# Float32 transposes and projections of an attention kernel, rewritten as products of 32 columns

## What is computed

```python
# x: (16, 512, 128) float32; H, dk = 16, 8
h = layernorm(x)
Q, K, V = (h @ Wq.T + bq), (h @ Wk.T + bk), (h @ Wv.T + bv)      # split into heads
scores = einsum('bhld,bhrd->bhlr', Q, K) * scale + einsum('bhld,lrd->bhlr', Q, rel_k)
attn = softmax(scores, axis=-1)
out = einsum('bhlr,bhrd->bhld', attn, V) + einsum('bhlr,lrd->bhld', attn, rel_v)
x = x + out @ Wo.T + bo
...
x = x + experts(layernorm(x))        # 2 shared experts, 2 of 8 routed ones
```

## Time and profile before

| | |
|---|---|
| median of 3 runs | 2068.07 us (2067.51 to 2069.0) |
| profiled execution | 2070.57 us, its span 2068.8 us |
| TensorE busy | 2037.4 us, 98% of the span, 37378 matmul records |
| DVE, ACT, POOL busy | 1605.3, 1507.0, 1212.4 us |
| granted TensorE clock, mean | 0.996 |

### The profile page before, as it was taken

The page is one execution under the profiler, slowest core; times in us unless marked ns, Lnnn a source line. Parts: engine busy times, 40 slices in busy tenths (PEclk is TensorE's granted clock), DMA queues, the critical chain, the costliest instruction groups (busy, mean ns, idle before and its releaser), DMA issues.

```text
span 2068.8 us, 86886 instructions
## 1 busy us (share of the span) xinstructions
PE 2037.4 (98%) x37378; PEld 1512.6 (73%) x37378; DVE 1605.3 (78%) x3788; ACT 1507.0 (73%) x3333; POOL 1212.4 (59%) x1283
## 2 busy tenths in 40 slices
PE   5999999999999999999999999999999999999999
PEld 3777777777777777777777777777777777777777
DVE  5877897788778877877897788778886767676765
ACT  3767676777677776667667666666666888888887
POOL 4554464456445544554455446444443898989888
PEclk8999999999999999999999999999999999999999
DMA  4212211221221122112211321223122221222120
GB/s 112 74 54 67 76 48 55 76 65 53 56 80 55 49 66 73 56 46 69 76 53 46 84 67 46 57 73 67 46 54 50 27 31 23 33 27 32 24 30 12
DMA packets 256658, 113.05 MB, mean 55 GB/s; under 512 B 143018, under 2 KB 253492, under 8 KB 256276
## 3 DMA queue, kind: packets, MB, share of 16 engines
q1 hardware_dynamic: 255796, 107.10, 21.3%
q10 hardware_dynamic: 480, 0.39, 0.1%
HBM read 83.34 MB, written 8.39 MB: 44 GB/s over the span
## 4 chain that ended last, share of the span: by engine, by line
PE 91%; DVE 4%; ACT 2%; POOL 1%; issue 1%; DMA 1%; SPq 0%; ACTq 0%; DVEq 0%; POOLq 0%
PE ps L1548 21%; PE ps L1483 12%; PE ps L1568 10%; PE ps L1490 8%; PE ps L1578 8%; PE ps L1501 7%; PE ps L1765 3%; PE ps L1767 3%; PE ps L1766 3%; PE ps L1747 3%; PE ps L1749 3%; PE ps L1748 3%; PE ps L1586 1%; ACT probs L777 1%; PE ps L1464 1%; DVE keys L1235 1%
## 5 line engine op out<-in xcount | busy, mean ns | idle before, releaser
L777 ACT ACTIVATE probs<-ps,neg_max 128x512 f32<-128x512 f32 x1024 | 690.4, 686 | 338.7 <-DVE neg_max L1003 338.6
L1003 DVE TENSOR_REDUCE neg_max<-ps 128x1 f32<-128x512 f32 x1024 | 635.8, 683 | 148.9 <-PE ps L1490 144.8
L549 POOL TENSOR_TENSOR stat_hi<-q_twice,mask8h 128x1024 f16<-128x1024 f16 x128 | 242.6, 1895 | 533.4 <-PE ps L1490 481.7
L1548 PE MATMUL ps<-const,probs 128*128 128x128 f32 x4096 | 497.3, 274 | 1.3 <-ACT probs L777 0.5
L1548 PEld LDWEIGHTS ps<-const,probs 128*128 128x128 f32 x4096 | 454.0, 141 | 29.5 <-issue 15.8
L1008 DVE COPY probs_t<-ps 128x512 f32<-128x512 f32 x512 | 339.9, 684 | 89.8 <-PE ps L1548 87.3
L767 ACT ACTIVATE probs_t<-ps 128x512 f32<-128x512 f32 x512 | 278.8, 595 | 131.8 <-PE ps L1548 129.5
L679 POOL TENSOR_TENSOR probs_t<-probs,probs_t 128x1024 f16<-128x1024 f32 x160 | 341.3, 2156 | 31.1 <-ACT probs_t L859 30.4
L1483 PE MATMUL ps<-keys,stat_hi 128*32 128x512 f16 x4096 | 317.4, 383 | 0.0
L1490 PE MATMUL ps<-rk_split,stat_rel 96*32 96x512 f16 (+2 forms) x4096 | 281.4, 340 | 0.0
L565 POOL TENSOR_TENSOR stat_rel<-q_rel,mask4h 96x1024 f16<-96x1024 f16 x128 | 250.6, 1958 | 49.7 <-PE ps L1490 30.6
(11 more groups left out here) (173 smaller groups left out, 2864.6 us busy)
## 6 DMA issues: line engine op xcount, KB each, us to landing
rv_step<-in_rv_win SPq DMA_DIRECT2D x128, 512.0 KB, 3.9
keys<-keys SPq DMA_DIRECT2D x56, 96.0 KB, 2.7
x_pair<-in_x SPq DMA_DIRECT2D x8, 512.0 KB, 4.4
rel_scratch<-rel_t SPq DMA_DIRECT2D x256, 16.0 KB, 3.2
x_pair<-in_x SPq DMA_DIRECT2D x16, 256.0 KB, 3.1
x_pair<-rel_scratch SPq DMA_DIRECT2D x64, 64.0 KB, 4.3
out<-keys SPq DMA_DIRECT2D x16, 256.0 KB, 2.3
q_twice<-q_hi SPq DMA_DIRECT2D x28, 128.0 KB, 3.0
```

The costliest lines, as they stand in the source:

```text
L777: nc.scalar.activation(probs[:, q, :], ps[:, i, :], ACT.Exp, bias=neg_max[:, q:q + 1], accum_out=row_sum[parity][:, s * QUADS + q:s * QUAD ...
L1003: nc.vector.tensor_reduce(neg_max[:, q:q + 1], ps[:, i, :], op=ALU.max, axis=AX_X, negate=True).then_inc(max_done, 1)
L1548: last = nc.tensor.transpose(ps[:, bank, rt * P:(rt + 1) * P], probs[:, q, rt * P:(rt + 1) * P], ident)
```

## The change

Every float32 transpose of the attention part becomes four float32 products, each with 32 columns of the block as the stationary operand and the identity as the moving one, which write 32 partitions each (new function `transposed`). The three projections are cut in the same way into products of 32 stationary columns: one product of 512 moving columns becomes four of 512, and one of 128 becomes four of 128. The block `rel_o` loses its upper half, which only held zeros, so its transpose is now two products. relative_queries (float16) keeps its transposes, and so do the transposes of the experts' part.

```diff
-        rel_o = sb("rel_o", [P, 4, 32])
+        rel_o = sb("rel_o", [P, 2, 32])
...
+            def transposed(out, rows):
+                for g in range(rows.shape[1] // 32):
+                    last = nc.tensor.matmul(out[32 * g:32 * g + 32, :], rows[:, 32 * g:32 * g + 32], ident, start=True, stop=True, skip_group_check=True)
+                return last
+
             def rows_t(pair, half, bank):
...
-                    last = nc.tensor.transpose(ps[:, bank, t * P:(t + 1) * P], x_pair[:, half * 4 + t, :], ident)
+                    last = transposed(ps[:, bank, t * P:(t + 1) * P], x_pair[:, half * 4 + t, :])
...
-                nc.tensor.matmul(ps[:, bank, :], wk_s[:], xn_t[:, b * L:(b + 1) * L], start=True, stop=True).then_inc(proj_done, 1)
+                for g in range(4):
+                    last = nc.tensor.matmul(ps[32 * g:32 * g + 32, bank, :], wk_s[:, 32 * g:32 * g + 32], xn_t[:, b * L:(b + 1) * L],
+                                            start=True, stop=True, skip_group_check=True)
+                last.then_inc(proj_done, 1)
...
-                    last = nc.tensor.transpose(ps[:, bank, l * D:(l + 1) * D], rows, ident)
+                    last = transposed(ps[:, bank, l * D:(l + 1) * D], rows)
...
-                    last = nc.tensor.matmul(ps[:, bank, t * D:(t + 1) * D], xn_t[:, b * L + t * P:b * L + (t + 1) * P], wv_s[:],
-                                            start=True, stop=True)
+                    for g in range(4):
+                        at = b * L + t * P + 32 * g
+                        last = nc.tensor.matmul(ps[32 * g:32 * g + 32, bank, t * D:(t + 1) * D], xn_t[:, at:at + 32], wv_s[:],
+                                                start=True, stop=True, skip_group_check=True)
...
-                        last = nc.tensor.transpose(ps[:, bank, rt * P:(rt + 1) * P], probs[:, q, rt * P:(rt + 1) * P], ident)
+                        last = transposed(ps[:, bank, rt * P:(rt + 1) * P], probs[:, q, rt * P:(rt + 1) * P])
...
-                nc.tensor.transpose(ps[:, AV_BANK, 3 * P:4 * P], rel_o[:].rearrange("p a r -> p (a r)"), ident).then_inc(rel_tr, 1)
+                transposed(ps[0:64, AV_BANK, 3 * P:4 * P], rel_o[:].rearrange("p a r -> p (a r)")).then_inc(rel_tr, 1)
```

More of the change, by code:

```diff
@@ L275, in attention_ffn @@
         SETUP_FIRST, SETUP_DVE = 6, 9
-        SETUP_POOL = 11
+        SETUP_POOL = 10
         POOL_LINKS = 10
@@ L502, in _ @@
             nc.gpsimd.memset(half_pow[:], -0.5).then_inc(setup_pool, 1)
-            nc.gpsimd.memset(rel_o[:], 0.0).then_inc(setup_pool, 1)
             nc.gpsimd.memset(e_const[:], math.e).then_inc(setup_pool, 1)
@@ L1031, in reduce_relative @@
                 dve.wait_ge(rel_tr, START + pair * STEPS + s)
-                nc.vector.tensor_reduce(rel_o[:, 0:2, :].rearrange("p a (g h) -> p (a g) h", h=DK), r_masked[:].rearrange("p g l h -> p g h l"),
+                nc.vector.tensor_reduce(rel_o[:].rearrange("p a (g h) -> p (a g) h", h=DK), r_masked[:].rearrange("p g l h -> p g h l"),
                                         op=ALU.add, axis=AX_X).then_inc(rel_reduced, 1)
@@ L1438, in project_keys @@
                 pe.wait_ge(xn_t_ready, START + pair * 2 + b + 1)
-                nc.tensor.matmul(ps[:, bank, :], wk_s[:], xn_t[:, b * L:(b + 1) * L], start=True, stop=True).then_inc(proj_done, 1)
+                for g in range(4):
+                    last = nc.tensor.matmul(ps[32 * g:32 * g + 32, bank, :], wk_s[:, 32 * g:32 * g + 32], xn_t[:, b * L:(b + 1) * L],
+                                            start=True, stop=True, skip_group_check=True)
+                last.then_inc(proj_done, 1)
             def project_queries(pair, b, bank):
-                nc.tensor.matmul(ps[:, bank, :], wq_s[:], xn_t[:, b * L:(b + 1) * L], start=True, stop=True).then_inc(proj_done, 1)
+                for g in range(4):
+                    last = nc.tensor.matmul(ps[32 * g:32 * g + 32, bank, :], wq_s[:, 32 * g:32 * g + 32], xn_t[:, b * L:(b + 1) * L],
+                                            start=True, stop=True, skip_group_check=True)
+                last.then_inc(proj_done, 1)
             def natural_queries(pair, b, bank):
```

## The result

The changed kernel takes 2514.41 us (median of 4 runs, 2513.56 to 2517.63) against 2067.9 us before (2067.51 to 2069.0): a ratio of 1.2161, interval 1.214 to 1.2182. It is slower, by 446.5 us of the medians; the forecast of 2495 us was 19 us short, and its range of 2450 to 2550 us holds the result. The profiled execution took 2513.56 us, its span is 2511.8 us, its clock 0.996 as before.

A forecast was written before the change was run, and what follows sets the result against it. TensorE was taken to bound the attention rounds; +448.0 us for two-instruction products, less saved entries and small piece terms, gave +426.8 us on the profiled 2070.57 us, so 2495 us from the median, range 2450 to 2550 us.

The forecast's parts named there:

- TensorE bounds the attention part: From 60 to 1586 us TensorE is busy 1524 of 1526 us, so its gains or losses move the end equally.
- Two instructions for a float32 product, 27.3 ns each among four tiles (+448.0): Probabilities' transposes: 128 instructions take 3.50 us per round instead of 1.75 us, +448.0 us in 256 rounds.
- Rivals 1 and 3: Respectively: a product is one instruction like the transpose (2033 us, 3%); it costs four passes against one (3391 us, 1%).
- Entries saved (-22.7): No change of width ahead of the transposes: 0.15 us saved in each of 151 rounds without a piece, -22.7 us.
- values (-3.7): project_values, 16 times: 1.10 us becomes 32 instructions in 0.87 us, -3.7 us.
- keys and queries (-5.8): project_keys and project_queries, 32 times: 1.05 and 1.06 us become 8 instructions in 0.87 us, -5.8 us.
- rows_t and natural_queries (+7.6): Transposes of these pieces, 16 times each: 0.58 and 0.68 us become 0.87 us, +4.6 and +3.0 us.
- Both far bounds of the projections (0.43 us and 1.74 us): Keys and queries projections: at float16 price, -20 us; with two passes that can't lie beside each other, +22 us.
- Behind relative_queries: Transposes after this full-width piece, 28 times, now have another shape: 0.12 us each, +3.4 us.
- The exit at nothing: From transposes to the next scores' low terms, the shape change costs as before: 0; if free, -31 us.
- rel_transposes at nothing: Two products, 4 instructions, cost 0.11 us as now without the entry; if two tiles pack worse, 0.22 us, +14 us.
- Rival 2: TensorE's instructions come too slowly: 2760 us if fetches aren't covered, 2584 us if issue lags a tenth; 7% together.

The follow-up runs named there:

- probs_only: Kernel before, with only the probabilities' transposes written as products of 32 columns: 2532.39 us against 2068.91, ratio 1.2241.
- f16_full: Kernel before, with float16 probabilities and each block one full-width float16 product with the identity: 1993.38 us, ratio 0.9635.
- projections_only: Kernel before, with only the key, query and value projections in tiles of 32 columns, all transposes as they were: 2066.34 us against 2069.84, ratio 0.9986.
- rel_four: Changed kernel, with `rel_o` widened by zeros to 128 columns, so its products fill four tiles instead of two: 2521.18 us, ratio 1.2187.
- tile_major: Changed kernel, with a quad's 16 products ordered by tile, 8 instructions in a row on each: 3622.93 us, ratio 1.7511.
- two_blocks: Changed kernel, with the products of two blocks at a time ordered by tile, 4 instructions in a row on each: 2537.42 us, ratio 1.2272.
- f16_products: Changed kernel, with float16 probabilities and a float16 identity in the probabilities' tiled products: 2024.37 us, ratio 0.978.

## Why the prediction was right, and where it was short

The sum was +426.8 us and the profiled executions differ by 443.0 us: 16.2 us short. The other 3 us of the 19 are the two profiled executions' distances from their medians (2.5 us above before, 0.9 us below after).

- **TensorE bounds the attention part.** Right: 1966 of 1969 us busy, and the part grew by what TensorE's groups grew by.
- **Two instructions for a float32 product, 27.3 ns each among four tiles (+448.0).** Right: x128 in 3.49 us, which makes +446.5 (256 x (3.494 - 1.75)). Rivals 1 and 3 fall by the same row. probs_only shows that this term carries the loss. The factor of two between product and transpose has a scale in f16_full: there full-width float16 products start every 56 ns, the float32 transpose takes 0.109 us, twice that, and a float32 product of 128 columns 0.22 us (the starts of L1464 before), four times.
- **Entries saved (-22.7), values (-3.7), keys and queries (-5.8), rows_t and natural_queries (+7.6).** Right as far as the rows tell: no group behind tiles shows an entry, 0.86 us for a projection of 512 columns (0.87 costed), x160 in 4.37 us, which is 3.49 and 0.87. projections_only measured 3.5 us of gain where the entries stay behind. Both far bounds of the projections (0.43 us and 1.74 us) are out.
- **Behind relative_queries.** Costed 0.12 us, measured 0.13 to 0.14.
- **The exit at nothing.** Right: from the last instruction of the transposes to the first of the low terms it is 202 ns, before 203 ns, and a round's 128 instructions up to that point take 3.597 us. Above the 3.494 us of 128 x 27.3 ns that is 0.103 us, where it had been 0.094; some 2 us in all. The bound of -31 us is out.
- **rel_transposes at nothing: the step that was mis-sized.** "4 x 27.3 ns = 0.11 us, what it costs now" assumed that four instructions always share four tiles. They lie on two, two on each, and cost 0.21 us: +0.10 us in 128 rounds, **+13 us**. It is the upper bound that the prediction named ("if two tiles alone don't pack as four do"), and rel_four shows the reason: the busiest tile is what counts, not the number of instructions.
- **Rival 2, stops of the issue, at 7% as a large one.** A small form of it is real: 4.4 us in the waits, none before. The cover of the fetches that the prediction reckoned with held at all but 11 of 534 places.

13 + 2 + 4 is 19 us against 16.2; 3.494 us in place of 3.50 takes 1.5 of the difference (256 rounds), and the rest is less than what a reading to 0.01 us in 256 rounds tells.

Expected and seen as well: the copies wait longer while TensorE doesn't wait for them, the experts' part is unchanged. The waits of ACT for the transposes grew more than DVE's (by 422 against 137 us).

## What to carry to other kernels

Count the records, not the calls: a float32 product is two instructions where the float32 transpose is one, and tiles of 32 columns win nothing when the full-width instruction already takes as long (0.109 us) as four tiled ones. With tiles side by side, cost a group by its busiest tile and alternate the tiles, at most four instructions in a row for one; a group that fills two of four tiles costs as much as one that fills all. When an edit makes the bounding engine cheaper, ask first who must have copied its last results: the float16 kernels lost part of their gain to waits, most of them for a copy of 0.70 us.

## What was not expected of the hardware

- **Products on different tiles start out of the order of the program.** These are starts in the changed kernel's trace at a `rel_transposes` (ns; the program lists the four of `rel_o` first):

```
1296559 rel_o    1296564 rel_o    1296572 probs    1296579 probs
1296669 rel_o    1296673 rel_o    1296705 probs    1296712 probs
```

  The first two of the probabilities start 0.1 us before the last two of `rel_o`. The records don't name a tile, but the distances fit only the two empty ones: the two rows of `rel_o` go on after 109 ns each. The last of `rel_o` is the one that signals. The Trainium skill ("TensorE: Matmul & The Clock Gate", Part 3) says that products are strictly in program order in start and end; for starts over column tiles this trace disagrees. The kernel loses nothing by it, but a signal on the last product of a group is safe only for what lies ahead of it on the same tile, unless ends are in order, which no run here tested.
- **About three instructions queue for one tile**, then all tiles behind are held up: 1.97 us for a quad with 8 in a row (tile_major), 3.58 us for a round with 4 in a row (two_blocks), 3.49 us with 2.
- **A float16 product of 32 by 128 columns takes 14 ns** of TensorE among four tiles (0.223 us for 16 starts), half of the float32 instruction's 27.3 ns.
- **TensorE's stops without a wait come at one place in every 256 records**, most of them 1.2 to 1.6 us after the end of a fetch of instructions, up to 2.3 us each. Kernels with denser instructions had more gaps there (41 in f16_products, 13 in the changed kernel, 2 before), lighter transfers fewer (5); the counts hold a few ordinary gaps.
